# The inverse deviation of sixteen heads, computed on GpSimd and VectorE in place of ScalarE and VectorE

## The reference, cut to what matters

```python
        p = jax.nn.softmax(scores, axis=-1)
        o = jnp.einsum('bhij,bjhd->bihd', p, v)
        o = o * jax.lax.rsqrt(jnp.mean(o * o, axis=-1, keepdims=True) + EPS) * o_norm_w
        return o.reshape(B, S, D) @ Wo.T
```

## Time and profile before

| | before |
|---|---|
| median of 3 runs | 696.13 us (696.03 to 697.79) |
| profiled execution, its own time | 697.43 us |
| its span, first to last instruction | 695.2 us |
| PE busy | 669.7 us, 96% |
| PEld busy | 581.7 us, 84% |
| DVE busy | 487.5 us, 70% |
| ACT busy | 424.8 us, 61% |
| POOL busy | 297.0 us, 43% |

### The profile page before, as it was taken

One profiled execution on the slowest core, in us unless ns is written; L12 is line 12 of the kernel. 1 busy time (PEld: TensorE's weight loads), 2 busy tenths in 40 slices (PEclk: granted clock), 3 DMA queues, 4 the chain that ended last, 5 costly groups with the idle time before them and its releaser, 6 DMA issues.

```text
span 695.2 us, 13848 instructions
## 1 busy us (share of the span) xinstructions
PE 669.7 (96%) x4756; PEld 581.7 (84%) x4756; DVE 487.5 (70%) x1418; ACT 424.8 (61%) x1100; POOL 297.0 (43%) x301
## 2 busy tenths in 40 slices
PE   5999999999999999999999989999989999999997
PEld 3777888888889888888888856666889999999997
DVE  6798867877877777777797877777465545644544
ACT  3856168788797878787763788988654222222221
POOL 0583155556464554542345228998333400400000
PEclk9999999999999999999999999999999999999999
DMA  8902044553535444343720000300300000000000
GB/s 324 355 0 99 1 131 121 162 167 118 167 117 158 123 153 124 115 141 108 308 114 0 1 2 1 108 1 3 122 1 1 1 10 8 1 16 1 1 16 17
DMA packets 26725, 59.43 MB, mean 85 GB/s; under 512 B 3146, under 2 KB 12748, under 8 KB 26272
## 3 DMA queue, kind: packets, MB, share of 16 engines
q1 hardware_dynamic: 23584, 50.35, 22.0%
q0 software_dynamic: 3072, 8.20, 3.6%
HBM read 48.24 MB, written 10.49 MB: 84 GB/s over the span
## 4 chain that ended last, share of the span: by engine, by line
PE 52%; ACT 5%; DVE 4%; issue 3%; POOL 1%; DMA 1%; DVEq 0%; ACTq 0%; POOLq 0%
PE bank L2262 11%; PE bank L2311 5%; PE bank L2285 5%; PE bank L2123 4%; PE bank L2170 2%; PE bank L2325 2%; PE bank L1961 2%; PE bank L2231 2%; PE bank L2027 2%; PE bank L2215 2%; PE bank L2242 2%; ACT sb L1206 2%; PE bank L2047 1%; PE bank L2018 1%; PE bank L2038 1%
## 5 line engine op out<-in xcount | busy, mean ns | idle before, releaser
L1068 ACT ACTIVATE sb<-bank,sb 128x256 f32<-128x256 f32 x128 | 59.6, 471 | 40.7 <-DVE sb L1566 38.8
L1566 DVE TENSOR_REDUCE sb<-bank 128x2 f32<-128x512 f32 x64 | 43.7, 683 | 47.9 <-PE bank L2027 47.6
L1272 ACT ACTIVATE h_parts<-sb 128x256 fp32r<-128x256 f32 x56 | 23.4, 418 | 71.3 <-DVE sb L1816 43.4
L2027 PE MATMUL bank<-sb 128*128 128x256 f32 x256 | 66.1, 381 | 0.0
L1807 DVE TENSOR_TENSOR sb<-sb,bank 128x256 f32<-128x256 f32 x56 | 23.5, 419 | 58.1 <-ACT sb L1235 58.1
L2262 PE MATMUL bank<-rounded,b_hi 128*128 128x256 f32 x224 | 63.1, 282 | 0.0
L2262 PE MATMUL bank<-rounded,b_lo 128*128 128x256 f32 x224 | 62.9, 281 | 0.0
L2262 PE MATMUL bank<-am_lo,b_hi 128*128 128x256 f32 x224 | 62.9, 281 | 0.0
L1235 ACT ACTIVATE sb<-bank 128x256 f32<-128x256 f32 x56 | 21.5, 383 | 62.3 <-PE bank L2262 62.3
L838 POOL DMA_INDIRECT expert_out<-sb x32 | 33.0, 1031 | 58.3 <-DVE sb L1508 45.0
L1075 ACT ACTIVATE sb<-sb 128x256 f32<-128x256 f32 x128 | 57.7, 503 | 0.1
(11 more groups left out here) (321 smaller groups left out, 1967.3 us busy)
## 6 DMA issues: line engine op xcount, KB each, us to landing
sb<-in_w_gate_up SPq DMA_DIRECT2D x32, 368.0 KB, 3.1
sb<-in_w_down SPq DMA_DIRECT2D x32, 256.0 KB, 2.7
sb<-in_w_pair SPq DMA_DIRECT2D x8, 704.0 KB, 4.0
expert_out<-sb SPq DMA_DIRECT2D x1, 4096.0 KB, 23.4
sb<-expert_out SPq DMA_DIRECT2D x8, 512.0 KB, 6.9
sb<-in_w SPq DMA_DIRECT2D x1, 1792.0 KB, 12.7
sb<-in_b SPq DMA_DIRECT2D x1, 1792.0 KB, 8.0
sb<-in_sw_up SPq DMA_DIRECT2D x1, 1536.0 KB, 8.8
```

The lines of the kernel that those rows point to most:

```text
L1068: act.activation(probs[:, u % 4, q, :], bank[3 + u % 2][:, q * S:(q + 1) * S], ACT.Exp, scale=-1.0, bias=row_min[:, u % 4, q:q + 1], accum ...
L1566: dve.tensor_reduce(row_min[:, u % 4, :], bank[3 + u % 2][:, :].rearrange("p (q n) -> p q n", q=QT), AX.X, ALU.min).then_inc(at_min, 1)
L2027: mm = pe.matmul(bank[3 + u % 2][:, q * S:(q + 1) * S], qb[i][:, h, b * S + q * P:b * S + (q + 1) * P], keys[:, h, b * S:(b + 1) * S], sta ...
```

## The change

The inverse deviation 1 / sqrt(v) is computed in another way. ScalarE's square root (L1301) and VectorE's reciprocal (L1846) go. GpSimd raises the variance tile to the power -0.5 elementwise with one `tensor_tensor`; it stands in its queue ahead of the low part of a2 tile 4 and waits for the mean (`on_step` at 3). The exponent comes from a tile `o_new`, filled with -0.5 by one more memset behind L900. VectorE, where the reciprocal stood, waits for the power (`on_act` at 3) and makes a Newton step y (1.5 - 0.5 v y y) in three `scalar_tensor_tensor` operations, each waiting for the one before. The waits that counted five fills now count six, and L1864 waits for `on_step` at 6.

```diff
-        o_var, o_sd, o_inv = sm.take(NT, H1), sm.take(NT, H1), sm.take(NT, H1)
+        o_var, o_new, o_inv = sm.take(NT, H1), sm.take(NT, H1), sm.take(NT, H1)
...
             pool.memset(v_last[:, :, D1:VW], 1.0).then_inc(kmean_set, 1)
+            pool.memset(o_new, -0.5).then_inc(kmean_set, 1)
...
-            pool.wait_ge(kmean_set, 5)
+            pool.wait_ge(kmean_set, 6)
             pool.wait_ge(rest_beats, NB - 1)
...
             for kind, n in weight_order:
                 if kind == "x1" and n > 1:
                     low_rank_parts(n)
+                if (kind, n) == ("a2", 4):
+                    pool.wait_ge(on_step, 3)
+                    pool.wait_ge(kmean_set, 6)
+                    pool.tensor_tensor(o_inv, o_var, o_new, ALU.pow).then_inc(on_act, 1)
                 raw, hi, lo = weight(kind, n)
...
-                if s == 3:
-                    act.wait_ge(on_step, 3)
-                    act.activation(o_sd, o_var, ACT.Sqrt).then_inc(on_act, 1)
...
-            dve.wait_ge(kmean_set, 5)
+            dve.wait_ge(kmean_set, 6)
             count(dve, 0, slice(0, QT * H1), beats_first, blk_beats, blk_count, 0)
...
                 if s == 4:
                     dve.wait_ge(on_act, 3)
-                    dve.reciprocal(o_inv, o_sd).then_inc(on_step, 1)
+                    dve.scalar_tensor_tensor(o_new, o_inv, -0.5, o_inv, ALU.mult, ALU.mult).then_inc(on_step, 1)
+                    dve.wait_ge(on_step, 4)
+                    dve.scalar_tensor_tensor(o_new, o_new, 1.0, o_var, ALU.mult, ALU.mult).then_inc(on_step, 1)
+                    dve.wait_ge(on_step, 5)
+                    dve.scalar_tensor_tensor(o_inv, o_new, 1.5, o_inv, ALU.add, ALU.mult).then_inc(on_step, 1)
...
-                    dve.wait_ge(on_step, 4)
+                    dve.wait_ge(on_step, 6)
```

## The result

The change makes the kernel slower: 714.72 us median (five runs, 714.38 to 715.98) against 696.03 us (five runs, 695.55 to 697.79), ratio 1.0267 with a 95% interval of 1.0253 to 1.0281, or 17.6 to 19.6 us. The forecast was 697.4 us in a range up to 703.9 us. The sign of the likeliest case (a little slower, within what can be measured) says nothing for it: the time lies outside the range.

What follows compares the result with a forecast made beforehand. TensorE, busy 96%, was taken as the bound, with its 2.09 us wait at hidden1(5) the place touched. The change X - 2.47 us with a power of X = 3.8 us gave +1.3 us: 697.4 us, range 694.0 to 703.9 us.

Steps and rivals of the forecast that it cites:

- The sign of the likeliest case: Whole kernel: likeliest was slightly slower, +1.3 us, within the 2.09 us a measurement can tell; chance 0.50 for that band.
- What bounds the kernel: TensorE, busy 96% of the span; only its waits change the time, here the 2.09 us wait at hidden1(5).
- ScalarE's part: End of step s = 3: two table loads and the root go, 2.97 us; Silu of (4, 0) starts 2.1 us sooner.
- The length of the power: GpSimd's power, length X: taken as 3.8 us, between 0.46 and 10.3 us.
- The rival of the long power: VectorE waits on GpSimd's power, delaying hidden1(5); break-even X = 2.47 us; chance 0.42 over 4.56 us, of it 0.12 over 10.3.
- The sum: At hidden1(5): start at 515.9 + X, so the time changes by X - 2.47 us; +1.3 us with X = 3.8.
- E + 0.29: VectorE's L1818: kept out until the power's end E = 514.0 + X, itself ending 0.29 us later.
- No term: TensorE's granted clock: a drop in a longer wait adds nothing, since 7 us idle at the start left it full.
- The memset and the counts: GpSimd's extra memset, some 0.3 us, falls in idle time and the waits for six are met: both nothing.
- The short power: GpSimd's power at 0.46 us: 694.1 us, or 693.7 without an a_lo wait; chance 0.30, of it 0.08 gaining over 0.3%.
- GpSimd ahead of L1812: Power starts before VectorE's L1812, putting L1812, rounding and L1818 behind it: +0.7 us, 698.1 us; chance 0.25, inside other cases.
- the change doesn't do what it says: ScalarE: a table load stays because another function needs it; time within 0.3 us of the forecast; chance 0.03.

Runs made afterwards that it cites:

- the copy run: Kernel before the change with ScalarE's square root replaced by a plain copy, reciprocal kept on VectorE: 695.05 us, ratio 0.9975.
- the half and the quarter: Changed kernel with the power on 64 or 32 of 128 elements, a plain product on the rest: 705.68 us (1.0132) and 700.11 us (1.0071).
- the filler: Changed kernel with 150 more matmuls on TensorE ahead of its wait for hidden1(5), into a bank nobody reads: 713.65 us, ratio 1.0241.
- the plain product: Changed kernel with GpSimd's power replaced by one plain product of the same two tiles: 693.65 us, ratio 0.9963.
- both versions: Kernel before, inverse root by VectorE alone (first guess, two Newton steps), products with the heads later, in two halves or three pieces: 693.83 us (0.9956), 692.63 us (0.9945).
- The powers at the end of the queue: Kernel before with four more powers, results unread, at the end of GpSimd's queue: 695.25 us, ratio 0.9991.

## Why the prediction was wrong, point by point

**What bounds the kernel** was right. TensorE's waits are the time, hidden1(5) was the one place where the change met it, and the wait there went from 2.09 to 20.0 us while the small ones stayed small (0.5 us for a_lo where it was 0.9, 0.8 us for L1877 as before).

**ScalarE's part** was right. The Silu of (4, 0) starts as soon as its tile is there (0.88 us of idling ahead of it where a table load stood), and the copy run shows the loads as its cause. In the rows of before no drain shows around a load (0.01 to 0.07 us to the next instruction), and no run here speaks against that.

**The length of the power is the step that failed.** The sum had X = 3.8 us and an upper end of 10.3 us; it measured 21.03 us, 5.5 times the one and twice the other. In the terms of the upper end, 36 passes at the price of a plain one, it is 74. The estimate carried the ratio of six from VectorE's reciprocal over to a power on GpSimd, where it does not hold, and the "upper" count of steps bounded nothing. In its place the runs show 160 ns for each element of a partition; what the engine does in them stays open. The rival of the long power named the mechanism, the place and the break-even, and gave 0.12 to a length of over 10.3 us; the range left just that out. A range that ends at a guess for a quantity that no row shows is too short on the side where the mechanism has no bound.

The figure of the GPSIMD Engine Reference in the Trainium skill (Performance versus the Vector engine), 12 cycles an element for data-dependent branching, gave an estimate of 1.3 us. At the page's clock of 1.2 GHz, 160 ns are, as an estimate, 192 cycles an element: sixteen times as much. The GPSIMD Engine Reference of the Trainium skill (Instruction dispatch) also has the once-only cost of some 6 us for a first call. It does not show in these executions: the only power of an execution takes 21.03 us, and the half and the quarter take their share of that.

**The sum** X - 2.47 us would have given +18.6 us with X = 21.03, and +18.7 was measured. That agreement is partly luck, since four of its terms were off. First, L1818 was to be kept out until the power's end (E + 0.29); it ran beside the power in 0.42 us, at 512.65. The SBUF — State Buffer page of the Trainium skill (Who interferes with whom) says that a VectorE instruction with two SBUF inputs contends with a GpSimd instruction that reads SBUF, and calls the contention an exclusive lock. The subtraction of the earlier trace rows agrees with that (1.49 us in place of 0.42), and the power does not: the operation ran wholly inside it in 0.42 us. Second, the Newton operations take 0.29 to 0.30 us each, not 0.35, and L1809 starts at 533.76, 0.91 us behind the power's end at 532.85; forecast was 1.39 us. These two made the sum 0.4 us too long (534.32 - 532.85 = 1.47 us against 1.90 us from the power's end to hidden1(5)). Third, the power began sooner. The trace of after is 1.95 us ahead of that of before here (TensorE's last ready matmul ends at 514.33 and 516.28), so its 511.82 is 513.77 on the scale of the forecast, which had 514.0. The three make 0.66 us, and the wait is 20.0 us where X - 0.4 gives 20.6.

**The clock** was the fourth, and a wrong step of its own. "No term" cost 1.7 to 1.8 us, so the trace's bill is 18.6 - 0.66 + 1.8 = 19.7 us. The argument was that TensorE stood for 7 us at the start of the span with the clock at full. The row is right and the conclusion is not: with the engine in work before it, 5.0 us of waiting brought the clock down to 1.2 GHz, and the filler kept it up.

The kernel before may pay this too. Of 41 executions of it taken beside the experiments, 18 have a mean granted clock of 1.000 and a median of 695.65 us, and 23 have 0.997 or 0.998 and a median of 697.37 us, 1.7 us more. The four kernels in which the wait of 2.09 us is gone or 0.68 us long (the plain product, the copy and both versions) have no such execution in 29. The powers at the end of the queue, which keep that wait, have 3 in 10. So its wait seems to let the clock fall in some executions and not in others. No trace of such an execution was kept, so where the clock fell is not shown. Against the 695.65 us alone, the copy for the root gains 0.6 us, the plain product 2.0, and the two versions 1.8 and 3.0 us.

**The memset and the counts**: nothing, as forecast; the plain-product run has them all and gains 0.37%.

**The rivals.** The short power is what the plain product played through: 693.65 us for the 694.1 (or 693.7) us forecast, with 0.66 us for the operation where 0.46 was taken. GpSimd ahead of L1812 did not happen: L1814 at 511.69 took 0.48 us and the power began at 511.82. That the change doesn't do what it says did not happen either.

## What to carry to other kernels

An operation whose length no row shows should be priced by one run of it in an idle queue before it is put ahead of a wait; where that can't be had, the range on its side stays open. A wait of several microseconds on TensorE has a second price, the granted clock behind it (1.2 to 1.8 us here). Count for a moved operation both who waits for its result and what is queued behind it: here the one cost 20.0 us and, with it out of the way, the other 16.4 us. To take a table switch off a tight engine, look for an engine that can do the same in plain operations and for a step in which it frees nobody: seven short operations of VectorE gained 3 to 4 us where one power of GpSimd lost 19.

## What the runs showed of the hardware that was not expected

- A power of two float32 tiles on GpSimd takes 160 ns for each element of a partition (5.5 to 5.7, 10.8 and 20.8 to 21.0 us for 32, 64 and 128), and the same for 8 partitions, as the fourth power of an execution, as for 128, as the first (20.82 and 20.83 us). A plain product of 128 elements took 0.66 us.
- Beside it VectorE's operations with two SBUF inputs keep their length (0.42 us), unlike beside a subtraction (1.49 us).
- TensorE's granted clock fell to 1.2 GHz during waits of 5.0, 10.05, 16.44 and 20.0 us, and not in the profiled wait of 2.09 us; it came back while TensorE was already at work, which made the stretch behind the wait 1.2 us longer after 5.0 us, and 1.8 us after 10.05 and 20.0 us.
- A first guess of the inverse root, by a multiplication and an addition on the bits of a float32 tile read as a whole number, is one operation of 0.22 us on VectorE for 128 elements.
